# Two softmax attention layers on one core: score maxima as an operand row written by DMA, operand stacks joined by DMA, one product a head, and rounding remainders split over two engines

## The reference, cut to what matters

```python
# third layer (L2_attn)
q, k, v = split(x @ w_qkv.T)                     # 16 heads of 8
logits = einsum('bhsd,bhtd->bhst', q, k) / sqrt(8)      # causal mask, softmax
out = einsum('bhst,bhtd->bhsd', probs, v) @ w_out.T
# fourth layer (L3_attn)
c_kv = x @ W_kv_down
k_rope = rotary(c_kv @ W_k_rope); q_rope = rotary(x @ W_q_rope)   # width 32, shared by the heads
scores = q.k (per head, width 8) + q_rope.k_rope;  scores / sqrt(40)   # causal mask, softmax
# fourth feed-forward (L3_ffn): 8 experts, top 2, and a shared expert
shared = gelu(x @ ws1 + bs1) @ ws2 + bs2
```

## Time and profile before

| | us |
|---|---|
| median of 3 runs | 2612.24 (2610.24 to 2615.01) |
| the profiled execution | 2591.79 |
| its span, first to last instruction | 2590.0 |
| PE busy / share of the span | 2029.6 / 78% |
| ACT busy | 1590.5 / 61% |
| DVE busy | 1579.7 / 61% |
| POOL busy | 1141.4 / 44% |
| mean granted TensorE clock | 0.879 of 2.4 GHz |

### The profile page before, as it was taken

One profiled execution on the slowest core, in us unless ns is written; L12 is line 12 of the kernel. 1 busy time (PEld: TensorE's weight loads), 2 busy tenths in 40 slices (PEclk: granted clock), 3 DMA queues, 4 the chain that ended last, 5 costly groups with the idle time before them and its releaser, 6 DMA issues.

```text
span 2590.0 us, 66263 instructions
## 1 busy us (share of the span) xinstructions
PE 2029.6 (78%) x23246; PEld 1391.6 (54%) x23247; DVE 1579.7 (61%) x3648; ACT 1590.5 (61%) x3690; POOL 1141.4 (44%) x930
## 2 busy tenths in 40 slices
PE   1553899999999788437889886853899999997993
PEld 0223566666666566334555554633566666665662
DVE  2236788787887888764554454766444544443775
ACT  0231577676777455206988897530788888886552
POOL 0002577664555233314854554330466654333552
PEclk9785899999999899856787786985999999998997
DMA  8900000020000111200020000220000000000224
GB/s 224 170 0 0 12 17 17 18 77 3 2 2 2 41 46 47 82 24 14 22 67 2 2 2 6 53 62 8 11 17 18 16 12 2 2 2 10 64 62 124
DMA packets 109678, 88.19 MB, mean 34 GB/s; under 512 B 11240, under 2 KB 95816, under 8 KB 109424
## 3 DMA queue, kind: packets, MB, share of 16 engines
q1 hardware_dynamic: 97840, 60.82, 10.3%
q0 software_dynamic: 11584, 23.91, 2.7%
HBM read 45.26 MB, written 39.43 MB: 33 GB/s over the span
## 4 chain that ended last, share of the span: by engine, by line
PE 44%; DVE 21%; ACT 14%; issue 12%; POOL 6%; DMA 2%; DVEq 1%; SPq 1%; ACTq 0%; POOLq 0%
PE duo L1023 9%; PE mo L1023 9%; PE misc L1023 8%; PE ob L1023 6%; PE acc L1023 6%; PE pt L1023 4%; ACT qT L865 3%; POOL v L643 3%; ACT v L903 3%; ACT v L902 2%; DVE nmax L2084 2%; DVE v L1805 2%; DVE region L2087 1%; DVE nmax L1974 1%; ACT L902 1%
## 5 line engine op out<-in xcount | busy, mean ns | idle before, releaser
L643 POOL TENSOR_TENSOR v<-v 128x768 f16<-128x768 f32 x256 | 419.6, 1639 | 545.5 <-ACT v L903 544.4
L638 POOL TENSOR_TENSOR v<-v 128x512 f16<-128x512 f32 x256 | 290.3, 1152 | 259.2 <-DVE region L2087 259.0
L865 ACT ACTIVATE qT<-small_ident,nmax 128x128 f16<-128x128 f32 x1024 | 328.9, 404 | 58.7 <-DVE nmax L1974 57.5
L665 POOL DMA_INDIRECT results<-probT,dest_no x202 | 217.2, 1075 | 330.2 <-ACT probT L704 290.9
L1973 DVE TENSOR_REDUCE nmax<-duo 128x2 f32<-128x256 f32 x256 | 108.4, 423 | 391.5 <-PE duo L1023 391.1
L1023 PE MATMUL ob<-wm,v 128*128 128x9 f16 (+1 forms) x5856 | 255.8, 180 | 82.7 <-POOL v L643 62.9
L1023 PEld LDWEIGHTS ob<-wm,v 128*128 128x128 f16 x5856 | 222.7, 98 | 144.4 <-POOL v L643 84.3
L964 ACT ACTIVATE v<-mo 128x512 f32<-128x512 f32 x256 | 153.4, 599 | 159.3 <-PE mo L1023 159.3
L1023 PE MATMUL duo<-kT,wm 128*128 128x256 f16 x1212 | 173.3, 280 | 54.8 <-DVE kT L1793 28.8
L2084 DVE TENSOR_REDUCE nmax<-duo 128x2 f32<-128x512 f32 x256 | 164.8, 685 | 83.4 <-PE duo L1023 83.4
L1023 PE MATMUL mo<-qT,kT 64*128 64x256 f16 (+1 forms) x2240 | 200.6, 271 | 0.0
(11 more groups left out here) (279 smaller groups left out, 4726.6 us busy)
## 6 DMA issues: line engine op xcount, KB each, us to landing
prob<-slot_rows SPq DMA_DIRECT2D x101, 130.0 KB
qT<-results SPq DMA_DIRECT2D x40, 256.0 KB, 3.1
slot_rows<-prob SPq DMA_DIRECT2D x4, 1300.0 KB, 20.6
slot_rows<-prob SPq DMA_DIRECT2D x4, 1235.0 KB, 22.2
xd<-in_L_ffn_w_dram SPq DMA_DIRECT2D x2, 2048.0 KB, 12.1
results<-probT,dest_no POOLq DMA_INDIRECT x202
slot_rows<-xd,slot_no POOLq DMA_INDIRECT x160, 2.4
x<-in_L_attn_x_dram SPq DMA_DIRECT2D x8, 256.0 KB, 4.6
```

What stands on the lines that cost most here:

```text
L638: pool.tensor_tensor(p16[:, p % 2, h, 1, :], p32[:, h, :], p16[:, p % 2, h, 0, :], ALU.subtract)\
L643: pool.tensor_tensor(p16_2[:, p % 2, 1, :], p32_2[:, p % 2, :], p16_2[:, p % 2, 0, :], ALU.subtract)\
L665: pool.indirect_dma_start(out=results[layer], out_offset=bass.IndirectOffsetOnAxis(ap=dest_no[:, 2 * b + t:2 * b + t + 1], axis=0), in_=y_ ...
L865: ins = act.activation(diag2[:, p % 2, n // 2, n % 2, :], small_ident[:, :], ACT.Copy, scale=nmax4[:, p % 2, n:n + 1])
```

## The change

All of it is in attention of layers 2 and 3.

- **Stacks.** `select`, `stack` and `pick_rows` go. SP's new `feed_attention` joins each group's stacks by DMA, `refill(i, g)`: in layer 2 25 DMAs a group (one of 4 rows, 24 of 8 rows of 1 KB), in layer 3 26 (two of 104 rows by four heads, 24 of 8 rows). A refill waits until the previous chunk's scores of that group are done; PE waits for it in `maxima` (`stack_in[g]`); ACT and DVE wait in `parts_free` (step 3) for the refills of groups 2 and 3 before they overwrite `parts`.
- **One product a head.** In layer 3 a head's stack has all 128 rows: rotated part, maxima row and the head's 24 rows. The shared product of `scores` and `maxima` goes.
- **Maxima as a row.** `diagonals` and the products with `sixteen16` go. DVE writes the negated maxima in 16 bits (`nm16`). Every second step PE transposes those of two steps to 4 rows (`turn_maxima`), DVE copies them to SBUF (`turn_rows`), and ACT issues a DMA (`send_rows`) that writes them as the row of `q_stack` or `head_q` that meets a row of ones in the key stack.
- **Order.** PE: `scores(p)`, `turn_maxima` (even p), `average(p - 1)`, `maxima(p + 6)` in layer 2 or `(p + 4)` in layer 3. ACT: first head's exponentials, `send_rows`, second head's. The preparation moves to steps 3 to 8, the shared expert to steps 9 to 13, its addition to step 14.
- **Low halves.** `pair_low` stays on POOL in even steps and is DVE's in odd ones.
- The load of layer 3's expert weights moves from the start of layer 2's attention to its chunks 3 and 4.

```diff
-        SELECT_AT = {0: (2, 3), 2: (4,), 4: (5,), 6: (6,), 8: (7,)}
-        SHARED_AT = {1: 0, 3: 1, 5: 2, 7: 3}
-        DOWN_AT = {4: 0, 5: 1, 7: 2, 8: 3}
-        PREPARE = range(9, 14)
+        SHARED_AT = {9: 0, 10: 1, 11: 2, 12: 3}
+        DOWN_AT = {10: 0, 11: 1, 12: 2, 13: 3}
+        PREPARE = range(2, 10)
+        LEAD = {2: 6, 3: 4}
...
+        def rows_ahead(layer, p, more):
+            e = (p + LEAD[layer] - 2) // 2
+            if p % 2 or e < 0:
+                return None
+            return (0, e) if e < 8 else (1, e - 8) if more else None
...
+                def refill(i, g):
+                    if i:
+                        s_full.wait(sp, stage, i - 1, 8 * g + 7)
...
+                    if layer == 2:
+                        put(q_stack[0:P:GROUP, g, :], k_stack[1:5, 0, :])
+                        for j in range(4):
+                            own = parts[GROUP * g + 8 * j:GROUP * g + 8 * j + 8, :, :]
+                            for stack, rows in ((k_stack, (2, 2, 3)), (q_stack, (0, 1, 0))):
+                                for r, n in enumerate(rows):
+                                    at = GROUP * j + 8 * r + 8
+                                    put(stack[at:at + 8, g, :], own[:, n, :])
...
 pool:
-                        else:
+                        elif p % 2 == 0:
                             pair_low(i, p)
 act:
-                def diagonals(i, p):
-                    nmax_made.wait(act, stage, i, p)
-                    for n in range(4):
-                        ins = act.activation(diag2[:, p % 2, n // 2, n % 2, :], small_ident[:, :], ACT.Copy,
-                                             scale=nmax4[:, p % 2, n:n + 1])
+                def send_rows(i, e):
+                    g, b = e // 2, e % 2
+                    nm_turned.wait(act, stage, i, e)
...
+                        act.dma_start(q_stack[0:P:GROUP, g, own], nm_rows[:, b, :]).then_inc(nm_in[b], 16)
...
+                def parts_free(i):
...
+                            act.wait_ge(stack_in[g], stack_count(layer, i))
...
-                        exps(i, p)
-                        if p + 2 < STEPS:
-                            diagonals(i, p + 2)
...
+                        exps(i, p, 0)
+                        at = rows_ahead(layer, p, more)
+                        if at:
+                            send_rows(i + at[0], at[1])
+                        exps(i, p, 1)
 pe:
+                def turn_maxima(i, e):
+                    nmax_made.wait(pe, stage, i, 2 * e + 1)
...
+                        ins = mm(nm_bank[qt], nm16[:, e % 2, 4 * qt:4 * qt + 4], ident_h[:, :], True, True)
+                    ins.then_inc(nm_full.sem, 1)
...
-                        scores(i, parity, p)
-                        if p + 2 < STEPS:
-                            maxima(i, parity, p + 2)
...
+                        scores(i, p)
+                        at = rows_ahead(layer, p, more)
+                        if at:
+                            turn_maxima(i + at[0], at[1])
                         if p >= 1:
                             average(i, parity, p - 1)
...
+                        at = ahead(layer, p, more)
+                        if at:
+                            maxima(i + at[0], at[1])
 dve:
+                def pair_low(i, p):
+                    p_high.wait(dve, stage, i, 2 * p + 1)
+                    dve.tensor_tensor(p16_2[:, 1, 1, :], p32_2[:, 1, :], p16_2[:, 1, 0, :], ALU.subtract)\
+                        .then_inc(low_odd.sem, 1)
+                def turn_rows(i, e):
+                    nm_full.wait(dve, stage, i, e)
...
+                    dve.tensor_copy(nm_rows[:, e % 2, :].rearrange("p (q c) -> p q c", q=2), src).then_inc(nm_turned.sem, 1)
...
+                        at = rows_ahead(layer, p, more)
+                        if at:
+                            turn_rows(i + at[0], at[1])
...
+                            maxima(i + at[0], at[1])
+                        if p % 2:
+                            pair_low(i, p)
...
                             prepare(i + 1, 1 - parity, p)
```

More of the change, by code:

```diff
@@ L933, in attention @@
                     prepare(0, 0, p)
-                diagonals(0, 0)
-                diagonals(0, 1)
+                for p in range(-LEAD[layer], 0):
+                    at = rows_ahead(layer, p, True)
+                    if at:
+                        send_rows(*at)
                 chunks1(act, chunk)
@@ L1277, in maxima @@
+                def turn_maxima(i, e):
+                    nmax_made.wait(pe, stage, i, 2 * e + 1)
+                    if layer == 2:
+                        at_step(nm_turned, pe, stage, i, e - 1)
+                    for qt in range(2):
+                        ins = mm(nm_bank[qt], nm16[:, e % 2, 4 * qt:4 * qt + 4], ident_h[:, :], True, True)
+                    ins.then_inc(nm_full.sem, 1)
+                def maxima(i, p):
                     g, b, jj = pair2(p)
                     if p % 4 == 0:
-                        stacked.wait(pe, stage, i, 2 * g + 1)
+                        pe.wait_ge(stack_in[g], stack_count(layer, i + 1))
@@ L1280, in maxima @@
                     at_step(nmax_made, pe, stage, i, p - 1)
+                    if layer == 3 and p % 2 == 0:
+                        at_step(nm_turned, pe, stage, i, p // 2 - 1)
                     q0, k0 = SEQ * b, SEQ * b
-                    if layer == 3:
-                        q, k = after["q"][parity], after["k"][parity]
-                        for h in range(2):
-                            mm(duo[:, h, 0:P], q[:, q0:q0 + P], k[:, k0:k0 + P], True, False)
-                            mm(duo[:, h, P:LINE], q[:, q0 + P:q0 + SEQ], k[:, k0:k0 + SEQ], False, False)
@@ L1339, in turn_o @@
                     o_made.wait(pe, stage, i, 3)
[L1340 to L1341 removed]
+                    if layer == 3:
+                        sh_added.wait(pe, stage, i)
+                    elif i < NCH - 1:
+                        proj_read_v.wait(pe, stage, i + 1, 2)
                     for t in range(TILES):
@@ L1404, in attention @@
                     prepare(0, p)
-                maxima(0, 0, 0)
-                maxima(0, 0, 1)
+                for p in range(-LEAD[layer], 0):
+                    at = rows_ahead(layer, p, True)
+                    if at:
+                        turn_maxima(*at)
+                    maxima(*ahead(layer, p, True))
                 for i in range(NCH):
@@ L1895, in attention, with parts_free @@
                     dve.memset(v[:, :, 1, :, 8:SLOT], 0.0).then_inc(v_ones2, 1)
+                blank_rows = (k_stack[:, :, :], q_stack[:, :, :]) if layer == 2 else \
+                    (after["k"][0][HEAD0:P, :], after["q"][0][HEAD0:P, :])
+                for a in blank_rows:
+                    dve.memset(a, 0.0).then_inc(stack_zero, 1)
+                dve.wait_ge(stack_zero, 2 * (layer - 1))
+                if layer == 2:
+                    for j in range(4):
+                        ins = dve.memset(k_stack[GROUP * j:GROUP * j + 1, :, :], 1.0)
+                else:
+                    ins = dve.memset(after["k"][0][HEAD0:HEAD0 + 1, :], 1.0)
+                ins.then_inc(stack_set, 1)
+                def parts_free(i):
+                    if not (isinstance(i, int) and i == 0):
+                        for g in (2, 3):
+                            dve.wait_ge(stack_in[g], stack_count(layer, i))
                 def take(ins):
@@ L2007, in chunk @@
                             scale_o(i - 1, 3)
-                        for n in SELECT_AT.get(p, ()):
-                            stack(i, n)
+                        at = ahead(layer, p, more)
+                        if at:
+                            maxima(i + at[0], at[1])
+                        if p % 2:
+                            pair_low(i, p)
                         if p == 2 and begun:
+                            if layer == 3:
+                                sh_added.wait(dve, stage, i - 1)
                             add(acc_full, x_made, i - 1, 0)
-                        if p == 8 and layer == 3:
-                            if begun:
-                                x_made.wait(dve, stage, i - 1)
+                        if p == 14 and layer == 3:
                             add(sh_down, sh_added, i, FB - 1)
@@ L2025, in attention @@
                     prepare(0, 0, p)
-                maxima(0, 0)
-                maxima(0, 1)
+                for p in range(-LEAD[layer], 0):
+                    at = rows_ahead(layer, p, True)
+                    if at:
+                        turn_rows(*at)
+                    maxima(*ahead(layer, p, True))
                 chunks1(dve, chunk)
```

319 lines of the change are left out of this document (173 added, 146 removed).

## The result

The changed kernel takes 3110.13 us (median of 4 runs, 3109.30 to 3113.41) where the kernel before, on the same chip, takes 2611.46 (4 runs, 2610.24 to 2615.01): ratio 1.191, 95% interval 1.189 to 1.193. It is slower by 499 us. The forecast was 2654, with a range to 2735: the sign was right, the size was not.

What follows compares the result with a forecast made beforehand. ACT was taken to bind, with a longer loop of waits replacing it. Layer 2 +44, layer 3 -3 and expert weights +1 on 2591.79 gave 2634, and 20.5 more for the median gave 2654 us; range 2575 to 2735.

Steps and rivals of the forecast that it cites:

- What hides: SP's 100 (104) DMAs a chunk, 36 to 38 us at 0.36, 48 at 0.475, stay under a chunk of 53.
- The second rival: SP's stream binds from 0.53 us an issue on; at 0.60, 66 and 81 us a chunk, 2854 in all; chance 0.08.
- The rule weighed against the change: Skill's advice to join small DMAs, about 2.0 us fixed each: SP's stream would bind; the forecast held it hidden.
- The loop: Two steps through waits of PE, DVE, ACT and POOL: 6.58 us, 3.29 a step, where a clean step was 2.68.
- ACT's issue: In `send_rows`, ahead of the second head's exponentials: issue of the DMA 0.33 us after a hop of 0.05.
- The clock: PE's half clock adds 0.42 us in two steps; taken for half of layer 2's steps, 13 us.
- the third rival: PE's clock stays at 1.2 GHz: +14 us in layer 2, 23 and 24 in layer 3, 2715 in all; chance 0.12.
- 443: Layer 2 in us without its later start: 421 for steps, 13 half clock, 5 DVE's low part in step 3, 4 drain.
- 528: Layer 3 in us without its later start: 421 for steps, 50 shared expert, 47 preparation, 5 half clock, 5 drain.
- The starts: First exponentials come some 18 us later in layer 2 and 11 later in layer 3, behind refills and first maxima.
- the first rival: The rows come in time, so ACT does not stand in `send_rows`: 2.6 us a step, 2461 in all; chance 0.16.
- POOL's sends of expert rows fit in its odd steps: In POOL's odd steps, the sends of expert rows were counted among what hides, with no time of their own.

Runs made afterwards that it cites:

- e1_thin: The changed kernel with refills of chunks 1 to 7 copying one head slot in four (other scores wrong): 2797.6 us, one run; before 2603.3.
- e5_via_memory: The changed kernel with head parts written to device memory and each group's stacks fetched by a few larger DMAs: 2685.07 us, ratio 1.037 to the kernel before.
- e8: The changed kernel with stacks via device memory, all low halves on POOL, maxima ahead of average, `send_rows` behind second head's exponentials: 2585.89 us, ratio 0.9995 to before.
- e4: The kernel before with each step's diagonals in layers 2 and 3 made by one DVE instruction instead of four of ACT: 2630.07 us, ratio 1.0096.
- e12: The kernel before with two of a step's four diagonals made by DVE, one instruction each, and two by ACT: 2645.78 us, ratio 1.0135.
- e2: The kernel before with thirteen series of DMAs issued by SP during layer 2, differing in rows, size or ends: 2607.3 us, one run; before 2603.3.

## Why the prediction was wrong, point by point

**The step that failed is the first sentence of "What hides".** "SP issues 100 (104) DMAs a chunk: 36 to 38 us at 0.36, 48 at the 0.475 of 128 rows, under a chunk of 53." Issues of 8 rows from device memory were taken for issues of 8 rows from SBUF. The earlier trace rows hold loads only, and no row of before showed a DMA with both ends in SBUF. This was an unknown operation, and by the forecast's own way of working it needed a bound from far away; 0.475 was the dearest of a kind that it did not belong to. It measured 0.667, and 0.95 for the two large ones of a group in layer 3: 67 to 68 us a chunk in layer 2 and 81 to 82 in layer 3, where chunks without the stall take 59.7 and 68 to 72 (e1_thin). So the issues were not hidden, and `parts_free`, which the forecast had put at nothing, became the wait that sets the chunk.

**The second rival was the right one, at a chance of 0.08.** Its sum (stream, landing and the time until the next parts are ready; 66 and 81 us a chunk at 0.60) is the mechanism that the trace shows, and the measured 0.667 lies above its threshold of 0.53 us an issue. At 0.667 its terms are 66.7 + 2 + 4 = 73 in layer 2, where 73 was measured, and about 81 + 2 + 17 = 100 in layer 3, where it was 102 to 111: landing and preparation took 22 to 26 us there, not 19. What it left out is the start: the first chunk's 100 issues stand ahead of everything, 45 us later instead of 18, and 28 instead of 11 between the layers.

**The rule weighed against the change was the better guide.** The advice of the Trainium skill, "DMA: Bandwidth & Descriptors", section "Rules for kernel authors", to join small transfers pointed to the side that came out; the rows that I set against it came from transfers of another kind. (The 2.0 us that its section on the anatomy of one DMA gives are for DMAs that GpSimd issues; these are SP's.) The size was not the reason, though: 8 x 4 KB issues as slowly as one row of 1 KB, and 128 rows of SBUF to SBUF as slowly as 8.

**The rest can be read in e5_via_memory,** where the stream is gone, 1.037 of its before; 2654 was 1.016 of 2612.
- *The loop.* Right in its order and its terms: VectorE's low half 0.95 (0.96 forecast), the rows' copy 0.41 (0.42), the reductions, GpSimd's 1.64, the exponentials. ACT's issue was too small: 0.52 in layer 2 and 0.59 in layer 3 (forecast 0.33 and 0.25, upper bound 0.43): 64 x 0.19 = 12 us and up to 64 x 0.34 = 22. These DMAs too have both ends in SBUF, but no run gave ACT another kind to compare. (The lower values add up to 5.86, not 5.88; nothing hangs on it.)
- *The clock.* "I take it for half of the steps": it was 1.2 GHz in almost all of layer 2 (0.52 to 0.58 in every kernel with the new loop), as the third rival had it: 13 us more. With the 12 above, 443 becomes 468. The windows of the earlier trace rows and the forecast's 443 and 528 hold the drain behind the last exponential, 4 and 5 us, which the windows here leave out: 464, where e5 shows 465.7, and in layer 3, where the mean clock was 0.83, 528 and at most 22 less 5, 545, where it shows 544.8. That it meets so closely is in part luck: in layer 2 two clean steps are 7.21 us as in that sum, but the chunks with preparation cost 11 us more than clean steps, not 5, and the last chunk, which prepares nothing, 7 less.
- *The starts.* 21 us later ahead of layer 2 (18), 16 more ahead of layer 3 (11), in e5.
- *"The rows come in time",* the first rival, didn't occur in the changed kernel; e8, which has the maxima ahead of the average and the send behind the exponentials, takes 5.5 us for two clean steps of layer 2 (the rival had 5.1), but its preparation and starts leave it even with the kernel before.
- *"POOL's sends of expert rows fit in its odd steps".* In chunks 0 and 1 of layer 2, where they are sent, the changed kernel's steps are 4.3 us long instead of 3.6; e5 has the same sends without the stream and has 3.6. In e1_thin, with the stream thinned from chunk 1 on, the steps of chunk 1 alternate between 3.6 and 4.0. So the sends fit alone and not beside SP's stream; what they meet there no run tells.

**What bounds the kernel before.** The forecast began with ACT as the engine that binds. Taking work off it gave a loop of waits that is longer, as forecast; whether it would be shorter with nothing put in its place is open (e4, e12).

## What to carry to other kernels

Count the DMAs that a loop issues and price them by their two ends before anything else: where both are in SBUF, an issue on SP cost 0.63 to 0.67 us here for 1 to 128 plain rows, and a buffer that is refilled by a hundred of them is held for that long, so that the chunk becomes the stream plus the time in which the stream's input is made. A detour through device memory with 12 or 20 larger DMAs a chunk instead of 100 small ones took four fifths of the loss away. And an instruction given to a less busy engine still has to come in that engine's queue at a time when nobody waits: the shorter low half on VectorE and the diagonals on VectorE both lost against longer ones on engines where they stood apart.

## What the runs showed of the hardware

- SBUF to SBUF issues on SP 0.63 to 0.67 us apart from 1 x 1 KB to 128 x 1 KB and 8 x 4 KB (e2), 0.95 for 104 rows written to four heads (changed kernel); 0.34 for 8 rows and 0.46 to 0.47 for 32 and 128 where one end is device memory (e2); ScalarE's issue from SBUF to SBUF took 0.52 to 0.59.
- A VectorE instruction on SBUF that GpSimd's low half overlaps took 1.81 us instead of 0.69 (512 columns) and 1.12 instead of 0.28 (128 columns), and ended 0.54 or 0.08 us after GpSimd's (e4, e12); its reductions from PSUM kept their time.
